# The ternary weights of the second half, quantized in a stage of their own instead of between the passes of the first half

## What is computed

```python
# first half
xn = layernorm(x); v, g1, g2 = split(xn @ W_in + b_in, 3)
y = fft_conv(v, k0) * g1;  y = fft_conv(y, k1) * g2      # causal, 128 taps
x = layernorm(x + (x + y @ W_out + b_out))
# second half
def weight_quant(w):
    scale = 1.0 / clip(mean(abs(w)), 1e-5, None)
    return clip(round(w * scale), -1, 1) / scale
def bitlinear(x, norm_w, w):                      # rmsnorm, x rounded to 8 bits
    return activation_quant(rmsnorm(x, norm_w)) @ weight_quant(w).T
h = act_scale * relu(bitlinear(x, norm1_w, w1))**2 + act_bias   # w1: 4096 x 1024
x = layernorm(x + bitlinear(h, norm2_w, w2))                    # w2: 1024 x 4096
```

## Time and profile before

| | us |
|---|---|
| median of 3 runs | 3335.76 (3327.18 to 3339.68) |
| the profiled execution | 3352.62 |
| its span, core 6, the slowest | 3351.1 |
| the other cores' spans | 3313.5 to 3347.0 |
| busy: VectorE / TensorE / ScalarE / GpSimd | 1634.9 / 1435.2 / 786.9 / 23.9 |
| first half ends (last x' store lands) | 1635 |

### The profile page before, as it was taken

The page is one execution under the profiler, slowest core; times in us unless marked ns, Lnnn a source line. Parts: engine busy times, 40 slices in busy tenths (PEclk is TensorE's granted clock), DMA queues, the critical chain, the costliest instruction groups (busy, mean ns, idle before and its releaser), DMA issues.

```text
span 3351.1 us, 20130 instructions; the slowest of 8 cores (3313.5 to 3351.1 us)
## 1 busy us (share of the span) xinstructions
PE 1435.2 (43%) x4270; PEld 431.7 (13%) x4270; DVE 1634.9 (49%) x1763; ACT 786.9 (23%) x1164; POOL 23.9 (1%) x48
## 2 busy tenths in 40 slices
PE   1645545543334442233223555444445544344553
PEld 0111111111111110010000111111111111111110
DVE  2244454433333333234114666666666666666665
ACT  0000101100000000000003444444444444444442
POOL 0000000000000000000000000000000000000000
PEclk9877776766666666666556676665667666666765
DMA  3432121112221112311550010000000000000000
GB/s 81 158 116 90 54 90 61 41 49 74 75 75 57 52 52 66 75 50 54 103 108 10 17 25 22 22 23 22 22 18 24 23 23 22 22 22 18 24 22 25
DMA packets 213810, 166.48 MB, mean 50 GB/s; under 512 B 174777, under 2 KB 179642, under 8 KB 212667
## 3 DMA queue, kind: packets, MB, share of 16 engines
q1 hardware_dynamic: 208604, 149.46, 16.4%
q0 software_dynamic: 5088, 15.74, 1.7%
HBM read 100.09 MB, written 29.36 MB: 39 GB/s over the span
## 4 chain that ended last, share of the span: by engine, by line
DVE 40%; DMA 13%; PEldq 13%; issue 12%; SPq 9%; ACT 8%; PEld 3%; DVEq 2%; ACTq 1%; POOLq 0%
PEldq L175 12%; DVE g2s L895 11%; DMA wsf<-w 8%; SPq L1022 5%; DVE Pb L656 5%; DVE wqb L802 2%; ACT d2s L888 2%; DVE f2s L885 2%; DVE xq2o L901 2%; DMA xq2Tc<-xq2o 2%; DVE wgt L799 1%; DVE d2s L898 1%; DVEq L175 1%; DVE wsum L766 1%; SPq L850 1%
## 5 line engine op out<-in xcount | busy, mean ns | idle before, releaser
L1031 PE MATMUL yc<-wq2T,xq2Tc 128*128 128x512 bf16 x1024 | 412.4, 517 | 377.6 <-DMA xq2Tc<-xq2o 365.5
L993 PE MATMUL pj<-wq1T,xq1T 128*128 128x512 bf16 x1024 | 318.1, 441 | 478.9 <-DMA xq1T<-xq 434.4
L895 DVE SCALAR_TENSOR_TENSOR g2s<-d2s,g2s 128x1024 bf16<-128x1024 bf16 x368 | 451.0, 1226 | 45.3 <-issue 2.1
L665 PE MATMUL pj<-Pb,s_winv 128*128 128x512 bf16 x198 | 105.9, 603 | 574.4 <-DVEq L175 574.4
L515 ACT ACTIVATE st_mu<-st_mu 128x1 f32<-128x1 f32 x34 | 6.9, 203 | 942.8 <-DVEq L175 942.8
L1031 PEld LDWEIGHTS yc<-wq2T,xq2Tc 128*128 128x128 bf16 x1024 | 113.9, 116 | 665.5 <-issue 647.5
L993 PEld LDWEIGHTS pj<-wq1T,xq1T 128*128 128x128 bf16 x1024 | 99.0, 105 | 709.1 <-issue 645.1
L799 DVE TENSOR_SCALAR wgt<-wsf,nthrw 128x1024 bf16<-128x1024 f32 x64 | 48.2, 753 | 274.3 <-DMA wsf<-w 272.0
L1051 DVE TENSOR_TENSOR t2f<-t2f,nw2r 128x1024 f32<-128x1024 f32 x64 | 78.4, 1225 | 147.5 <-ACTq L175 139.6
L888 ACT ACTIVATE d2s<-f2s 128x1024 bf16<-128x1024 bf16 x64 | 67.6, 1056 | 300.9 <-DVEq L175 300.9
L598 PE MATMUL yc<-Wg,xnT 128*128 128x512 bf16 x576 | 136.7, 380 | 2.9
(11 more groups left out here) (179 smaller groups left out, 1862.8 us busy)
## 6 DMA issues: line engine op xcount, KB each, us to landing
wsf<-w SPq DMA_DIRECT2D x128, 512.0 KB, 4.7
sc_wq<-wqb SPq DMA_DIRECT2D x64, 256.0 KB, 2.3
wf<-W_in SPq DMA_DIRECT2D x8, 1536.0 KB, 7.8
xr<-x_own POOLq DMA_DIRECT2D x16, 512.0 KB, 4.0
xq2Tc<-xq2o SPq DMA_TRANSPOSE x512, 2.3
out<-outb SPq DMA_DIRECT2D x16, 512.0 KB, 2.7
sc_xp<-xp POOLq DMA_DIRECT2D x16, 256.0 KB, 2.3
xp<-sc_xp SPq DMA_DIRECT2D x16, 256.0 KB, 2.7
```

The source lines that it names most:

```text
L665: tiv = sch.op("tensor", (lambda wkey, pi, dc, mi_: lambda e: e.matmul(pshalf("pj", dc), cst[wkey][:], Pb[pi][:, dc * 512:(dc + 1) * 512], ...
L895: tn = sch.op("vector", (lambda lv: lambda e: e.scalar_tensor_tensor(gbuf[:, 0:width], dbuf[:, 0:width], 0.5 + lv, gbuf[:, 0:width], OP.is ...
L993: (lambda ss, dc, h: lambda e: e.matmul(pshalf("pj", h), xq1T[:, dc * 128:(dc + 1) * 128], wq1T[dc][:, ss * 1024 + h * 512: ss * 1024 + (h ...
L1031: (lambda k, q, oc, kb: lambda e: e.matmul(pshalf("yc1", oc), xq2Tc[kb][:, q * 128:(q + 1) * 128], wq2Tc[k * 8 + q][:, oc * 512:(oc + 1) * ...
```

## The change

`wsteps_gen` and its seven steps per pass are gone. In their place a function `wquant` runs once for w1 and once for w2, behind a barrier after the whole first half. It works on whole rows: 32 tiles of 128 x 1024 (512 KB) for w1, 8 tiles of 128 x 4096 (2 MB) for w2, with two buffers `wqf` where there were four, and with the loads on the GpSimd queue instead of the sync queue. The stores stay on the sync queue. The buffers now lie where those of the first half were. Apart from this, each matmul of the first projected tile waits for its own slice of `Wg`, where the first waited for all eight.

```diff
     ar.push()
+    wqf = [A(f"wqf{i}", [128, HID], F32) for i in range(2)]
+    wqb = [A(f"wqb{i}", [128, HID], BF16) for i in range(2)]
+    wgt = A("wgt", [128, HID], BF16)
...
-                         tok_wg_ev[7] if j == 0 and oc == 0 and c == 0 else None),
+                         tok_wg_ev[c] if j == 0 else None),
...
-        for _ in range(7):
-            next(wgen, None)
...
     barrierA = sch.barrier()
+    def wquant(wdram, ntiles, width, wsum, scdram, mc_t, wtcol):
+        toks_sum = []
+        prev = [F("wqf0"), F("wqf1")]
+        for i in range(ntiles):
+            buf = i % 2
+            td = sch.op("gpsimd", (lambda i, buf: lambda e: e.dma_start(
+                out=wqf[buf][:, 0:width], in_=wdram[i * 128:(i + 1) * 128, :]))(i, buf),
+                barrierA + ((prev[buf],) if prev[buf] else ()), "DQ")
+            ts_ = sch.op("vector", (lambda i, buf: lambda e: e.reduce_sum(
+                wsum[:, i:i + 1], wqf[buf][:, 0:width], axis=AX,
+                apply_absolute_value=True))(i, buf), (td,), "V")
+            prev[buf] = ts_
+            toks_sum.append(ts_)
...
+        for i in range(ntiles):
+            buf = i % 2
+            td = sch.op("gpsimd", (lambda i, buf: lambda e: e.dma_start(
+                out=wqf[buf][:, 0:width], in_=wdram[i * 128:(i + 1) * 128, :]))(i, buf),
+                ((prev_d[buf],) if prev_d[buf] else (toks_sum[-1],)), "DQ")
+            tg_ = sch.op("vector", (lambda i, buf: lambda e: e.tensor_scalar(
+                wgt[:, 0:width], wqf[buf][:, 0:width], nthrw[:], None,
+                OP.is_lt))(i, buf), (td, tnt, F("wgt")), "V")
+            tq_ = sch.op("vector", (lambda i, buf: lambda e: e.scalar_tensor_tensor(
+                wqb[buf][:, 0:width], wqf[buf][:, 0:width], thrw[:],
+                wgt[:, 0:width], OP.is_gt, OP.subtract))(i, buf),
+                (tg_, F(f"wqb{buf}")), "V")
+            free["wgt"] = tq_
+            prev_d[buf] = tq_
+            tst = sch.op("sync", (lambda i, buf: lambda e: e.dma_start(
+                out=scdram[i * 128:(i + 1) * 128, :], in_=wqb[buf][:, 0:width]))(i, buf),
+                (tq_,), "DS")
...
+    tok_wq1 = wquant(w1, NW1T, D, wsum1, sc_wq1, mc1b, 0)
+    tok_wq2 = wquant(w2, NW2T, HID, wsum2, sc_wq2, mc2b, 1)
```

More of the change, by code:

```diff
@@ L291, in build_nc @@
     ar.pop()
[L293 to L298, removed]
+    ar.push()
+    wqf = [A(f"wqf{i}", [128, HID], F32) for i in range(2)]
+    wqb = [A(f"wqb{i}", [128, HID], BF16) for i in range(2)]
+    wgt = A("wgt", [128, HID], BF16)
+    totb = A("totb", [128, 1], F32)
+    thrw = A("thrw", [128, 1], F32)
+    nthrw = A("nthrw", [128, 1], F32)
+    w_peak = ar.cur
+    ar.pop()
     ar.push()
@@ L754, in build_nc @@
[L754 to L808, removed]
-                out=stsl, in_=wqb[buf % 2][:]))(stsl, buf), (tq_,), "DS")
-            free[f"wqb{buf % 2}"] = tst
-            w_store_toks[m].append(tst)
-            yield
@@ L831, in build_nc @@
             emit_xload(i + 2)
[L833 to L834 removed]
     barrierA = sch.barrier()
[L837 to L838 removed]
+    def wquant(wdram, ntiles, width, wsum, scdram, mc_t, wtcol):
[11 more added lines that the diff above has]
+            toks_sum.append(ts_)
+        trow = sch.op("vector", (lambda: lambda e: e.reduce_sum(
+            wtot[:, wtcol:wtcol + 1], wsum[:, 0:ntiles], axis=AX))(),
+            tuple(toks_sum), "V")
+        tap(f"wsum_{wtcol}", wsum, (trow,))
+        tap(f"wtot_{wtcol}", wtot, (trow,), freekey="wtot")
+        tmm = sch.op("tensor", (lambda: lambda e: e.matmul(
+            ps["ps_g"][:, 0:1], cst["ones_sq_f32"][:], wtot[:, wtcol:wtcol + 1],
+            start=True, stop=True))(), (trow, F("ps_g"), tok_cst["ones_sq_f32"]), "T")
+        tev = sch.op("vector", (lambda: lambda e: e.tensor_copy(
+            totb[:], ps["ps_g"][:, 0:1]))(), (tmm, F("totb")), "V")
+        free["ps_g"] = tev
+        tap(f"totb_{wtcol}", totb, (tev,), freekey="totb")
+        tmc = sch.op("vector", (lambda: lambda e: e.tensor_scalar(
+            mc_t[:], totb[:], 1.0 / NWELEM, 1e-5, OP.mult, OP.max))(), (tev,), "V")
+        free["totb"] = tmc
+        tth = sch.op("vector", (lambda: lambda e: e.tensor_scalar(
+            thrw[:], mc_t[:], 0.5, None, OP.mult))(), (tmc, F("thrw")), "V")
+        tnt = sch.op("vector", (lambda: lambda e: e.tensor_scalar(
+            nthrw[:], thrw[:], -1.0, None, OP.mult))(), (tth, F("nthrw")), "V")
+        prev_d = [None, None]
+        tlast = None
+        tstores = []
+        for i in range(ntiles):
[15 more added lines that the diff above has]
+                (tq_,), "DS")
+            free[f"wqb{buf}"] = tst
+            tlast = tst
+            tstores.append(tst)
+        free["thrw"] = tlast
+        free["nthrw"] = tlast
+        free["wqf0"] = prev_d[0]
+        free["wqf1"] = prev_d[1]
+        return tuple(tstores)
```

20 lines of the change are left out of this document (3 added, 17 removed).

## The result

| us | before | after |
|---|---|---|
| median (lowest to highest, runs) | 3340.3 (3327.2 to 3351.7, 10) | 3215.4 (3208.2 to 3221.5, 10) |
| the profiled execution | 3352.6 | 3210.4 |
| first half ends, core 6 | 1635 | 1113 |
| weights are ready, core 6 | inside the first half | 1488 |

The ratio is 0.9622, with an interval of 0.9603 to 0.9641. The change makes the kernel 125 us faster by the medians.

A forecast was written before the change was run, and what follows sets the result against it. Weight steps on the path bound the first half, mostly waits for loads behind stores in the in-order sync queue. Removing 525 us and adding a 370 us stage gives −155: 3335.8 to 3181, own range 3150 to 3225, wider range 3130 to 3255.

The forecast's parts named there:

- What goes, 525.0: Weight steps between first-half passes: VectorE's work and waits, 520.9 us, plus threshold chains, 4.1, all leave the path.
- the step of 155: Whole kernel: predicted gain of 155 us, worked out on the profiled execution and applied to the median of the runs.
- What is late next: First-half passes, behind the last projection copy: TensorE's transforms are done earlier, nothing is waited for, 525.0 counts in full.
- What comes, 370: New weight stage after the first half: sums and quantizing of w1 and w2 plus last store, 370 us.
- The sum: Whole kernel: 370 us added less 525 removed gives −155, from 3335.8 to 3181.
- Rival 1: Stage's quantizing: VectorE's `wgt` delays GpSimd's load issues, costing 21 us, time 3202; chance 0.11.
- Rival 2: Weight stage at its upper bound, landings 6.3 us and 222 GB/s: 496 us, time 3307; chance 0.13.
- rival 3: Weight stage with all cores streaming, slowest held at 147 GB/s: 617 us, time 3428, slower than before; chance 0.06.
- Rival 4: First-half passes: TensorE idles less, inverse transforms may run as fast as forward ones, gaining 35 us, time 3146; chance 0.08.
- Rival 5: Weight stage at its lower bound, landings 3.6 us and w2's stores free: 332 us, time 3143; chance 0.05.

The follow-up runs named there:

- Experiment 6: Kernel before with one small part each: w2 cut into contiguous pieces, 3320.5 us (ratio 0.994); finer waits on `Wg`, 3330.3 us (1.000).
- Experiment 4: Changed kernel with four `wqf` for two: 3140.5 us; with four `wqb` too and the load and store queues swapped: 3122.4 us.

## Why the prediction was right, and what was mis-sized

**What goes, 525.0.** This is the step that was mis-sized, in the sentence "everything that VectorE does or waits for in these steps". As a count of the trace it was right: on core 6 the first half ends at 1112.6 where it ended at 1635.1, 522.5 earlier. That it fits so well is in part luck: the blocks were 528.3 with the gaps at their edges, the first product came 6.1 earlier once they were taken out, and the passes got 11.5 longer. And the runs give 490. The span of core 6 without weights is 3351.1 - 2836.3 = 515 shorter, 10 less than 525, about the loss in the passes. From slowest core to slowest core it is 506, since another core then ends last. From median to median it is 490, since the profiled execution of before lay 16 us above its median. Summed over their blocks in the same trace, the steps were 499 to 533 us by core, and most on the three cores that ended last, 0, 4 and 6 (526 to 533). The spread sits in w2's quantizing: passes of 51.6, 47.4, 56.5 and 46.7 us there, against 44 to 47 on cores 3 and 5. Experiment 6 shows that it hangs on w2's pieces. I took the step of 155 over from the profiled execution to the median unchanged, though what made its last cores long was in the part that the change removes whole. A small misreading is beside it: the seven pieces from 864.92 to 906.26 are 5.9 us each and not 6.4, since the first finds its load landed; the sum did not use it.

**What is late next.** Nothing behind the copy, as said: the product follows it by 0.2 us. But that the 525.0 "count in full" put a term at nothing that measured 11.5 us: the passes did not stay the same. With the blocks of weight steps taken out, the 17 passes from the first product to the last residual sum took 848.0 us before and take 859.5. The groups say where, before and after:

```profile
L598 PE MATMUL pj<-Wg,xnT 128*128 128x512 bf16 x288 | 105.5, 532 | 72.1 <-DVEq L175 72.1
...
L618 DVE CAST proj<-pj 128x1024 bf16<-128x1024 f32 x16 | 19.6, 1225 | 111.0 <-PEq L175 111.0
L725 DVE SCALAR_TENSOR_TENSOR r_buf<-xr,pj 128x1024 f32<-128x1024 f32 x16 | 19.5, 1221 | 109.1 <-PEq L175 109.1
```

```profile
L598 PE MATMUL pj<-Wg,xnT 128*128 128x512 bf16 x288 | 110.3, 552 | 73.1 <-DVEq L175 73.1
...
L618 DVE CAST proj<-pj 128x1024 bf16<-128x1024 f32 x16 | 19.6, 1225 | 116.7 <-PEq L175 116.7
L725 DVE SCALAR_TENSOR_TENSOR r_buf<-xr,pj 128x1024 f32<-128x1024 f32 x16 | 19.5, 1221 | 111.9 <-PEq L175 111.9
```

VectorE waits 5.7 us longer for the first projected bank and 2.8 longer for the output product, whose matmuls take more time (532 ns, now 552, and 522, now 531). The kernel without the stage shows the same 859.9, so it comes from the missing steps and not from the stage. The timeline of TensorE shows what the slower and the faster matmuls have in common. Before, behind the seven sums, and in the second half of the first bank:

```profile
437.84 0.58 PE L665 MATMUL pj<-Pb,s_winv 128*128 128x512 bf16 x1 [12.05 <-DVEq L175]
...
476.36 2.38 PE L598 MATMUL pj<-Wg,xnT 128*128 128x512 bf16 x8
```

The same two places after:

```profile
421.29 0.38 PE L665 MATMUL pj<-Pb,s_winv 128*128 128x512 bf16 x1 [0.39 <-DVEq L175]
...
460.83 2.81 PE L598 MATMUL pj<-Wg,xnT 128*128 128x512 bf16 x8
```

It is the granted clock. Before, TensorE had been idle for 12 us and the inverse transforms ran at 0.50, the lower level (437.8 to 440.5). Now it has been idle for 0.4 us and the first three of them run at 0.98 (421.2 to 425.3). But the eight matmuls of the first bank that are shown ran at 0.78 (476.3 to 478.8) and now run at 0.67 (460.8 to 463.7), and the second eight of the output product at 1.00 and now at 0.84. The higher level comes back later in the pass than it did. The faster transforms gain nothing here, since TensorE waits for the next product of VectorE all the same (2.17 us before, 2.38 after); the slower matmuls are waited for. The inverse transforms as a group went from 603 to 566 ns. What moves the clock within the pass was not tried.

**What comes, 370.** Right in the total and nearly so in its parts:

| | forecast | core 6 |
|---|---|---|
| w1, sums (first load to last sum) | 97 | 95.7 |
| w1, quantizing | 118 | 117.6 |
| w2, sums | 62 | 64.8 |
| w2, quantizing | 89 | 92.1 |
| last store | 5 | 4.7 |

Together that is 374.9, and 369 by the medians. The tiles came 2.9 and 3.5 us apart in w1 and 7.2 and 10.5 in w2 (10.3 forecast), the last as pairs in rounds of 21 to 23 us. The landing of 2 MB was taken from 310 GB/s and came out as 12.2 us, not 9.1. The rate is 257 GB/s in w2's quantizing where I had let load and store fill 310. Experiment 4 shows that this is no limit of the memory, with 309 GB/s in the same part. With two buffers the two loads of a round go out 7 us apart (1410.23 and 1417.38) and share most of their way, and VectorE then has two tiles in a row.

**The sum.** 522.5 less and 375.4 more are -147, and the second half took 1718.2 us after 1716.0: -145 on core 6, and core 1 ended 2.6 later. From profile to profile it is -142. The rest to -125 is what is said of the first step: before's profile lay 12.3 us above its median, after's 5.0 below.

**The rivals.** Rival 1 is real as a mechanism and smaller than priced (21): three issues beside a long comparison are stretched from 0.53 to 2.0, 2.3 and 2.2 us, 4.9 us in all, and none beside the short ones of w1. No run isolates its cost; swapping the queues gives 26 us, mostly elsewhere. Rival 2 (496) and rival 3 (617) fall with 375 on the core and 173 to 258 GB/s, though all eight cores read at once; no core ended more than 17 us from another. Rival 4 has its premise right, the inverse transforms went from 603 to 566 ns, and its sign wrong: the passes lost 11.5 us. Rival 5 falls with a median landing of 3.9. The Trainium skill (DMA: Bandwidth & Descriptors, section Anatomy of one DMA) gives 3.2 us for 512 KB and 6.8 for 2 MB, from which the stage was estimated at 305 us; the trace disagrees with 3.9, 12.2 and 375.

What I missed is not in the sum but beside it. The prediction names the in-order queue as the reason of 272 us, and then credits its end to the move. The two parts had opposite signs.
